# Two-layer graph network on one core: gathers counted as landed two gathers later, none beyond the last tile, and an output stage spread over three engines

## What is computed

```python
edge_index = jnp.stack([src, dst])
# layer 0
msg = relu(concat([x[dst], x[src], edge_attr, u_per_node[dst]]) @ W1 + b1)
agg = segment_sum(msg, dst)
x = layernorm(x + relu(concat([x, agg, u_per_node]) @ W2 + b2))
# layer 1: attention with one weight matrix for each of 8 edge types
Z = einsum('ni,rio->nro', x, fc_weight)
e = relu(sum(concat([Z[src, etype], Z[dst, etype]]) * aw, axis=1))
alpha = softmax of e over the edges of one dst
x = layernorm(x + segment_sum(alpha * Z[src, etype], dst))
```

## Time and profile before

| | us |
|---|---|
| three runs, median (lowest to highest) | 4691.93 (4690.2 to 4699.62) |
| the profiled execution, its own time | 4689.66 |
| its span in the profile | 4687.6 |
| layer 0, first to last gather | 294 to 2298 |
| layer 1, first to last gather | 2582 to 4569 |
| output stage, first operation of DVE to the end of the span | 4625 to 4687.6 |
| busy in the span: PE, DVE, ACT, POOL | 78%, 66%, 28%, 64% |

### The profile page before, as it was taken

The page is one execution under the profiler, slowest core; times in us unless marked ns, Lnnn a source line. Parts: engine busy times, 40 slices in busy tenths (PEclk is TensorE's granted clock), DMA queues, the critical chain, the costliest instruction groups (busy, mean ns, idle before and its releaser), DMA issues. The chain is left out here.

```text
span 4687.6 us, 75265 instructions
## 1 busy us (share of the span) xinstructions
PE 3657.6 (78%) x18002; PEld 2990.4 (64%) x18002; DVE 3116.6 (66%) x9591; ACT 1296.4 (28%) x4292; POOL 3020.5 (64%) x3184
## 2 busy tenths in 40 slices
PE   1588788888788888888899577778787778788873
PEld 0565555656566666666676466667677777777773
DVE  4446666767677777777663566667676767777777
ACT  1010000000000000000132344455555555555552
POOL 0237777777777777777400777777777777777771
PEclk9755555555555555555565555555555555555555
DMA  3122222333333333333223222222232322322231
GB/s 80 56 57 64 65 65 64 70 64 70 64 70 68 69 69 69 68 69 67 45 95 145 63 55 53 55 55 55 55 56 55 58 55 55 58 55 58 55 57 31
DMA packets 294264, 297.24 MB, mean 63 GB/s; under 512 B 116497, under 2 KB 176069, under 8 KB 293799
## 3 DMA queue, kind: packets, MB, share of 16 engines
q0 software_dynamic: 101184, 107.08, 14.9%
q1 hardware_dynamic: 192663, 185.34, 14.0%
HBM read 255.43 MB, written 39.05 MB: 63 GB/s over the span
## 5 line engine op out<-in xcount | busy, mean ns | idle before, releaser
L661 POOL DMA_INDIRECT ring<-Ztab,idx x1568 | 1485.2, 947 | 785.0 <-issue 442.3
L661 POOL DMA_INDIRECT ring<-Btab,idx x1568 | 1486.0, 948 | 656.7 <-issue 455.5
L1171 PE MATMUL p_s<-ring,ohx 128*128 x3328 | 812.8, 423 | 379.0 <-issue 376.4
L1171 PEld LDWEIGHTS p_s<-ring,ohx 128*128 128x128 f32 x3328 | 740.4, 327 | 398.9 <-issue 398.9
L751 PE MATMUL p_m<-W1c,eaT 64*128 64x128 f32 x1664 | 659.8, 498 | 225.2 <-DMA eaT<-in_eaT_in 225.0
L759 PE MATMUL p_s<-msg,oh 128*128 128x64 f32 x3328 | 761.7, 424 | 92.5 <-ACT msg L733 91.7
L759 PEld LDWEIGHTS p_s<-msg,oh 128*128 128x128 f32 x3328 | 725.3, 330 | 142.6 <-issue 142.6
L751 PEld LDWEIGHTS p_m<-W1c,eaT 64*128 64x128 f32 x1664 | 415.2, 309 | 488.0 <-DMA eaT<-in_eaT_in 293.9
L792 DVE TENSOR_TENSOR p_t<-p_t,ring 128x64 f32<-128x64 f32 x1664 | 385.7, 232 | 457.0 <-POOLq L654 447.5
L733 ACT ACTIVATE msg<-p_t 128x512 f32<-128x512 f32 x208 | 124.2, 597 | 1903.7 <-DVE p_t L792 1903.7
L1260 DVE SCALAR_TENSOR_TENSOR XA<-XA,ff,p_s 128x65 f32 x1664 | 467.2, 281 | 123.7 <-DVE XA L1260 70.9
(11 more groups left out here) (199 smaller groups left out, 3305.4 us busy)
## 6 DMA issues: line engine op xcount, KB each, us to landing
drow<-drow_d SPq DMA_DIRECT2D x416, 256.0 KB, 3.4
eaT<-in_eaT_in SPq DMA_DIRECT2D x1664, 16.0 KB
Ztab<-Z_stage SPq DMA_DIRECT2D x24, 1072.0 KB, 4.3
ring<-Btab,idx POOLq DMA_INDIRECT x1568
ring<-Ztab,idx POOLq DMA_INDIRECT x1568
Btab<-B_stage SPq DMA_DIRECT2D x24, 128.0 KB, 2.0
out_x<-XA SPq DMA_DIRECT2D x6, 448.0 KB
idx<-ix_d SPq DMA_DIRECT2D x2, 784.0 KB, 4.4
```

The costliest lines, as they stand in the source:

```text
L661: e.indirect_dma_start(out=ring[:, t % RING, :], out_offset=None, in_=table[:, :], in_offset=bass.IndirectOffsetOnAxis(ap=idx[:, t:t + 1], ...
L1171: last = e.matmul(pS[s % 2][h][:, j % 4, :], OHx[:, s % 2, j, :], ring[:, bass.ds(t, 1), 0:D + 1], start=True, stop=True)
```

## The change

Three things. First, `gathers` waits for the transfers of group s - 1 not after the second gather of group s but after its fourth (or after the last one, where the last group is shorter). Second, it issues no gathers for the padding: 1563 instead of 1568 in each layer, the last group having three; the counts that `counted` waits for are adapted. Third, the output stage is written anew: POOL also adds x, ACT squares, and DVE keeps five operations a chunk, in a software-pipelined order in which the second half of one chunk alternates with the first half of the next; the mean and the reciprocal root lie in PSUM.

```diff
     def counted(s):
-        e.wait_ge(s_g[s % len(s_g)], 16 * O * (s // len(s_g) + 1))
+        tiles = min(O, NT - s * O)
+        before = sum(min(O, NT - i * O) for i in range(s % len(s_g), s, len(s_g)))
+        e.wait_ge(s_g[s % len(s_g)], 16 * (before + tiles))
         e.sem_inc(landed, 1)
 
-    for s in range(TO):
-        if s >= RT:
+    for t in range(NT):
+        s, j = divmod(t, O)
+        if s >= RT and j == 0:
             e.wait_ge(used, s - RT + BEHIND + 1)
-        for j in range(O):
-            t = s * O + j
-            e.indirect_dma_start(out=ring[:, t % RING, :], out_offset=None, in_=table[:, :],
-                                 in_offset=bass.IndirectOffsetOnAxis(ap=idx[:, t:t + 1], axis=0)).then_inc(s_g[s % len(s_g)], 16)
-            if s and j == 1:
-                counted(s - 1)
+        e.indirect_dma_start(out=ring[:, t % RING, :], out_offset=None, in_=table[:, :],
+                             in_offset=bass.IndirectOffsetOnAxis(ap=idx[:, t:t + 1], axis=0)).then_inc(s_g[s % len(s_g)], 16)
+        if s and j == min(3, NT - s * O - 1):
+            counted(s - 1)
     counted(TO - 1)
...
         @block.gpsimd
         def _(e):
+            e.wait_ge(s_den, 2)
+            for i in range(CH):
+                e.tensor_tensor(out=Y[:, sl(i), :], in0=A.acc1[:, sl(i), 0:D], in1=den[:, sl(i), :].to_broadcast([P, LNB, D]),
+                                op=ALU.mult).then_inc(s_raw, 1)
+                e.wait_ge(s_raw, i + 1)
+                e.tensor_tensor(out=Y[:, sl(i), :], in0=Y[:, sl(i), :], in1=A.x1[:, sl(i), :], op=ALU.add).then_inc(s_y, 1)
...
+            def centred(i):
+                e.wait_ge(s_y, i + 1)
+                e.tensor_reduce(out=mean[:, i, :], in_=Y[:, sl(i), :], axis=AXX, op=ALU.add).then_inc(s_mean, 1)
+
+            def subtracted(i):
+                e.wait_ge(s_mean, i + 1)
+                e.scalar_tensor_tensor(out=Y[:, sl(i), :], in0=over(mean[:, i, :]), scalar=-1.0 / D, in1=Y[:, sl(i), :],
+                                       op0=ALU.mult, op1=ALU.add).then_inc(s_sub, 1)
+
+            def varied(i):
+                e.wait_ge(s_sq, i + 1)
+                e.tensor_reduce(out=var[:, i, :], in_=SQ[:, i % 2, :, :], axis=AXX, op=ALU.add).then_inc(s_var, 1)
+
+            def inverted(i):
+                e.wait_ge(s_root, i + 1)
+                e.reciprocal(out=rstd[:, i, :], in_=var[:, i, :]).then_inc(s_rs, 1)
+
+            def scaled(i):
+                e.wait_ge(s_rs, i + 1)
+                e.tensor_tensor(out=A.x1[:, sl(i), :], in0=Y[:, sl(i), :], in1=over(rstd[:, i, :]), op=ALU.mult).then_inc(s_out, 1)
+
+
+            for i in range(CH + 1):
+                if 1 <= i <= CH:
+                    varied(i - 1)
+                if i < CH:
+                    centred(i)
+                if 1 <= i <= CH:
+                    inverted(i - 1)
+                if i < CH:
+                    subtracted(i)
+                if 1 <= i <= CH:
+                    scaled(i - 1)
...
+            def squared(i):
+                e.wait_ge(s_sub, i + 1)
+                if i >= 2:
+                    e.wait_ge(s_var, i - 1)
+                e.activation(SQ[:, i % 2, :, :], Y[:, sl(i), :], ACT.Square).then_inc(s_sq, 1)
+
+            def rooted(i):
+                e.wait_ge(s_var, i + 1)
+                e.activation(var[:, i, :], var[:, i, :], ACT.Sqrt, scale=1.0 / D, bias=A.epsb[:, 0:1]).then_inc(s_root, 1)
+
+            for i in range(CH):
+                squared(i)
+                rooted(i)
```

More of the change, by code:

```diff
@@ L1285, in phase_out @@
     LNB = 14
-    PAIRS = [(i, i + 1) if i + 1 < NB // LNB else (i,) for i in range(0, NB // LNB, 2)]
+    CH = NB // LNB
     with ExitStack() as ctx:
@@ L1290, in phase_out @@
         Y = sb("Yo", [P, NB, D], F32)
+        SQ = sb("SQo", [P, 2, LNB, D], F32)
         den = sb("den", [P, NB, 1], F32)
[L1292 to L1295, removed]
+        mean = bank(ctx, nc, "po_mean", [P, CH, LNB])
+        rstd = bank(ctx, nc, "po_rstd", [P, CH, LNB])
+        var = sb("var_o", [P, CH, LNB], F32)
+        s_den, s_raw, s_y, s_mean, s_sub, s_sq, s_var, s_root, s_rs, s_out, s_od = (sem("out_" + n) for n in (
+            "den raw y mean sub sq var root rstd out dma").split())
         block = ctx.enter_context(nc.Block())
@@ L1298, in phase_out @@
         sl = lambda i: slice(i * LNB, (i + 1) * LNB)
+        over = lambda st: st.unsqueeze(2).to_broadcast([P, LNB, D])
         @block.gpsimd
         def _(e):
-            e.wait_ge(s_den, 1)
-            for i in range(NB // LNB):
+            e.wait_ge(s_den, 2)
+            for i in range(CH):
                 e.tensor_tensor(out=Y[:, sl(i), :], in0=A.acc1[:, sl(i), 0:D], in1=den[:, sl(i), :].to_broadcast([P, LNB, D]),
-                                op=ALU.mult).then_inc(s_mul, 1)
+                                op=ALU.mult).then_inc(s_raw, 1)
+                e.wait_ge(s_raw, i + 1)
+                e.tensor_tensor(out=Y[:, sl(i), :], in0=Y[:, sl(i), :], in1=A.x1[:, sl(i), :], op=ALU.add).then_inc(s_y, 1)
@@ L1307, in _ @@
         @block.vector
         def _(e):
[L1309 to L1326, removed]
@@ L1328, in _ @@
-            for pair in PAIRS:
-                weave(*[chunk(i) for i in pair])
+            e.tensor_scalar(out=den[:, :, :], in0=A.acc1[:, 0:NB, D:D + 1], scalar1=1e-20, scalar2=None, op0=ALU.max).then_inc(s_den, 1)
+            e.wait_ge(s_den, 1)
+            e.reciprocal(out=den[:, :, :], in_=den[:, :, :]).then_inc(s_den, 1)
+            def centred(i):
+                e.wait_ge(s_y, i + 1)
+                e.tensor_reduce(out=mean[:, i, :], in_=Y[:, sl(i), :], axis=AXX, op=ALU.add).then_inc(s_mean, 1)
@@ L1340, in _ @@
             ov = A.out[0:(NB - 1) * P, :].rearrange("(b p) d -> p b d", p=P)
-            for i in range(NB // LNB):
-                e.wait_ge(s_o, i + 1)
+            for i in range(CH):
+                e.wait_ge(s_out, i + 1)
                 hi = min((i + 1) * LNB, NB - 1)
@@ L1345, in _ @@
             e.dma_start(A.out[(NB - 1) * P:N, :], A.x1[0:LAST, NB - 1, :]).then_inc(s_od, 16)
-            e.wait_ge(s_od, 16 * (NB // LNB + 1))
+            e.wait_ge(s_od, 16 * (CH + 1))
 class Arrays:
```

## The result

The changed kernel takes 4606.58 us (median of 4 runs, 4605.22 to 4610.21), the kernel before 4691.07 us (4 runs, 4685.01 to 4699.62): 84.5 us less, a ratio of 0.982 with a 95% interval of 0.9803 to 0.9837. The forecast of 4613 was 6 us too high; the range held. In the first session of experiments all kernels, the one before too, took some 6290 us, so the times of that session are compared with each other alone.

What follows compares the result with a forecast made beforehand. POOL's gathers were taken to bound layer 0 and layer 1 up to PE's last wait, a DVE chain the output stage. -43.8 - 13.8 - 19.9 = -77.5 from 4689.66 gives 4612.2, stated as 4613 us, range 4601 to 4636.

Steps and rivals of the forecast that it cites:

- Layer 0, the stalls: POOL's stalls before third gathers, 42 us in layer 0, should vanish with the later wait; taken as 41.5 us.
- Rival A: Gather queue: waiting only moves to before the fifth gather, as long as before; 4670 us in all; 6%.
- Rival D: Gathers' cadence rises behind more unlanded gathers; slower from 1.282 us a gather, 4746 us at 1.30; 2%.
- a constant shift of 2.5 us: Both layers: `landed` signalled two gathers later in every group, paid once at the end; 2.5 us, less in layer 0.
- The tail of layer 0: End of layer 0: later signal +1.25, two free steps of 16.57 us replacing 20.13; sum -2.3 us.
- Layer 1: Only stalls before PE's last wait for POOL count: 16.3 us less 2.5, so -13.8 us.
- a tie: Layer 1: PE's wait 32 steps earlier could become the last instead, 4.1 us earlier but gaining 3.9 less.
- Output stage: DVE sets the pace at 4.5 us a round; last scaling ends at 4663.5 instead of 4683.45, -19.9 us.
- Rival B: Output stage: engines still take turns, or ACT's turn is longer; gain 13.6 instead of 19.9, 4619 us; 12%.
- The table load: Output stage: ACT's 1.28 us load between first square and first root, by the row costing nothing.
- the estimate of 18.9: Output stage's gain if the table switch adds a 1.38 us drain, making the stage 1.0 us longer.
- Rival C: Consumers of layer 0 become its limit if a free step exceeds 9.4 us; 4634 if half the 42 is lost; 6%.

Runs made afterwards that it cites:

- c2: Kernel before, with a register clamp, and only the wait moved from behind the second to behind the fourth gather: 4636.6 us, ratio 0.9894.
- c3: Changed kernel, with a register clamp, the wait behind the first gather of a group instead of the fourth: 5109.2 us, ratio 1.0901.
- d3: Changed kernel, with a register clamp, the wait behind the eighth gather of a group instead of the fourth: 4608.4 us, ratio 0.9824.
- c1: Changed kernel whole, plus a clamp of the awaited group's register before the waits for `landed`: 4612.1 us, ratio 0.9843.
- d4: Changed kernel, with a register clamp, means and reciprocal roots of the output stage in SBUF instead of PSUM: 4616.5 us, ratio 0.9837.
- e0: Changed kernel whole with a register clamp, in the first session: 6274.3 us where the kernel before took 6296.4, ratio 0.9964.
- c4: Changed kernel, with a register clamp, PE keeping ring positions in four register sets in layer 1 instead of reloading: 4584.2 us, ratio 0.978.
- d1: Kernel before with nothing but the clamped register in the two waits for `landed`: 4698.2 us, ratio 1.0009.
- d2: Kernel before, with a register clamp, and the new output stage alone: 4672.5 us, ratio 0.9958.

## Why the prediction was right, and where it was off

**Layer 0, the stalls: right.** Forecast -41.5; from the first to the last gather 2004.0 us became 1955.4, less 6.2 for the five gathers: -42.4. c2 and c3 show the mechanism. Rival A (the stall moves along) is out: nothing waits before the fifth gather. Rival D too: a gap of 0.30 and a gather of 0.947 as before.

**The step that failed: "`landed` is told later by two gathers in every group, a constant shift of 2.5 us".** There is no such shift. Over the steps in which DVE waits, the first addition starts 2.11 us (median) after the end of the group's last gather before and 2.09 after; in the group at the end of layer 0, DVE adds at 2250.61, before the third gather, behind which the signal stands, starts at 2251.71. The landing sets the signal, not the place of the wait, as long as POOL's queue is ahead; d3 shows it even at the eighth gather. The forecast had taken the queue's place in the program for the time at which the signal goes out. The shift was put into two terms. The tail of layer 0 had +1.25 for it: forecast -2.3, measured -3.6 (-46.0 up to the last `msg`, of which -42.4 are the stalls). In layer 1, the forecast took 2.5 from 16.3: -13.8 for what was -17.6. With both taken back they come to -3.6 and -16.3. It made the forecast 3.8 us too high, and nothing cancelled it: the other errors, 1.3 us in layer 1 and 2.5 in the output stage, lie on the same side. All three are small beside the gain, which is why the forecast held.

**Layer 1: right in its mechanism.** PE's last wait for POOL in the changed kernel is at step 96, at 3490.88, one of the two places between which the forecast saw a tie; from there on steps take 9.39 us as before. From its first gather PE gets there 952.6 us into the layer, which is 965.5 less 12.9, where the forecast counted 13.1 us of stalls. Without the shift its own count for this place gives 13.1 + 4.1 = 17.2, near the 17.6 measured. Which wait is the last varies from run to run: with the same stalls gone it is at step 96 in c2 and at step 76 in c1 and d3.

**Output stage: right, one term too long.** A round is 4.23 us, not 4.5. The square was 0.95 as taken, but the turn from DVE to ACT took 0.03 us instead of 0.19 (4574.06 + 1.07 = 4575.13, and the next square stands at 4575.16 in the trace), and the two sums and the reciprocal 2.14 instead of 2.24. The 0.19 was read in the old stage, where DVE's queue told ACT by an instruction of its own behind the sum (releaser `DVEq L1319`); now the operation itself raises the semaphore. Six rounds shorter by 0.27 are 1.6 of the 2.5 us by which -19.9 fell short of -22.4; the first subtraction, 6.0 us into the stage rather than 6.3, and the stretch from the last one to the end, 4.9 rather than 5.4, are another 0.8. (The old stage had six long operations a chunk on DVE, not the five that the prediction names; no term rests on it.) Rival B is out: POOL's operations took 1.69 and 1.93, none 2.5. d4 gives its price, 9.2 us, more than the 6.3 that the forecast put between the two.

**The table load cost nothing.** It ends at 4573.18, the root starts at 4573.20, and DVE comes to the reciprocal at 4573.91, 0.4 us after the root. The drain of 1.38 us that the Trainium skill adds (ScalarE: Activation LUTs, What ACT_TABLE_LOAD costs) doesn't show here: the square ends at 4571.88, the load starts at 4571.90. The measurement decides, and the estimate of 18.9 by that page falls.

**Rival C** (consumers of layer 0 as limit) didn't occur in the sessions of 4690 us. It did in the first, where it took the whole gain of the wait: there a step of layer 0 took 14.6 us on average ((3341.0 - 295.6)/208 in the trace of e0), far over the 9.4 us from which it decides. The load of `eaT` that the forecast had named was part of it; DVE's late start behind PE, seen in the same traces, was not foreseen.

## What to carry to other kernels

Where one queue both issues transfers and waits for them to land, count what it has issued behind the awaited one: the queue must hold more work than the landing takes. Here the landing was told 2.1 us after the gather's end in the median and at most 3.8, and POOL needed 0.6 to start again, 2.7 to 4.4 in all; one gather behind it covers 1.55 us (0.30 and 1.25), two 2.8, four 5.3. One stalled in every group, two in 60 of 195, four in none. More distance cost nothing, up to the eight tried, since the signal still went out when the transfer had landed. Before counting a gain on such a queue, look at who waits for it in each stage, and until when: the same edit was worth some 50 us where its engine was waited for and nothing where others set the pace. Time that an engine spends on nothing visible, again and again before the same line, is worth a look at its register loads: keeping four sets of registers, in place of loading one again, gave another 28 us (c4).

## What was new of the hardware

POOL's queue can be seven gathers ahead of what its engine shows as started (d3). The padding at the end, whose gathers read one and the same row throughout, had landed 5.2 us after its end in layer 0 of the kernel before (4.5 to 4.9 in c2, d1 and d2), where others take 2.1; that the one row is the reason wasn't tried. Two broadcast operands of 14 elements a partition, moved from PSUM to SBUF, made a stage of 36.3 us 9.2 us longer (d4). And in one session SP took 6.5 to 12.6 us for eight issues that take 3.9 otherwise, and DVE started 2.26 us rather than 0.04 behind PE's last recorded matmul in layer 1, on a chip that didn't do so in another session, while a gather kept its 0.945 us.
